# Graph attention stage: per-wave softmax work spread over more steps, three banks of sums cleared by TensorE, gathers let go one by one

## What is computed

```python
q, k, v = (h @ Wq, h @ Wk, h @ Wv)            # each (n, H, 32)
e = jnp.sum(q[dst] * k[src], axis=-1) / np.sqrt(DK)
m = jax.ops.segment_max(e, dst, num_segments=n)
a = jnp.exp(e - m[dst])
z = jax.ops.segment_sum(a, dst, num_segments=n)
alpha = a / (z[dst] + 1e-09)
msg = v[src] * alpha[:, :, None]
agg = jax.ops.segment_sum(msg, dst, num_segments=n)
```

## Time and profile before

| | |
|---|---|
| median of 3 runs | 7516.76 us |
| the profiled execution, its own time | 7514.5 us |
| span of the profile | 7512.8 us |
| PE busy (share of the span) | 5151.3 us (69%) |
| DVE busy | 2817.6 us (38%) |
| ACT busy | 1775.8 us (24%) |
| POOL busy | 2144.2 us (29%) |
| granted TensorE clock, mean | 0.795 |

### The profile page before, as it was taken

How to read it: one execution, slowest core, us unless ns; L and a number is a source line. 1 busy time by engine, 2 the same in 40 slices (tenths; PEclk the granted TensorE clock), 3 DMA queues, 4 the chain that set the end, 5 groups by cost and what they waited for, 6 DMA issues and landing times. The chain is left out here.

```text
span 7512.8 us, 86978 instructions
## 1 busy us (share of the span) xinstructions
PE 5151.3 (69%) x21926; PEld 3443.6 (46%) x21975; DVE 2817.6 (38%) x6705; ACT 1775.8 (24%) x4567; POOL 2144.2 (29%) x2209
## 2 busy tenths in 40 slices
PE   3510959659783597956666666666667969898954
PEld 2410547315681146834444444444457844444433
DVE  4260679200423004155555545555534220202052
ACT  2210236000220002214444423444422210101020
POOL 3356010540244401414444305444300410000014
PEclk7555579769796697978888778888877989999966
DMA  0000023213562133637777527777611644243323
GB/s 14 1 1 1 1 93 140 81 59 112 166 198 78 64 104 99 198 128 249 233 230 234 175 69 246 242 236 230 185 50 40 201 152 150 105 137 116 112 71 113
DMA packets 484694, 960.56 MB, mean 128 GB/s; under 512 B 112649, under 2 KB 292468, under 8 KB 481718
## 3 DMA queue, kind: packets, MB, share of 16 engines
q1 hardware_dynamic: 324902, 640.53, 25.1%
q0 software_dynamic: 114208, 281.05, 12.8%
q10 hardware_dynamic: 45296, 35.56, 1.6%
HBM read 737.19 MB, written 219.73 MB: 127 GB/s over the span
## 5 line engine op out<-in xcount | busy, mean ns | idle before, releaser
L1180 PE MATMUL banks<-ring,xn 128*128 128x512 f32 (+1 forms) x3500 | 1445.0, 568 | 397.6 <-issue 277.4
L1180 PEld LDWEIGHTS banks<-ring,xn 128*128 128x128 f32 x3500 | 644.5, 196 | 1198.8 <-issue 1182.3
L1007 POOL DMA_INDIRECT rows<-pairs,idxr x832 | 866.3, 1041 | 912.2 <-DVE prod L2022 637.0
L383 POOL DMA_INDIRECT dst_table<-nodes_pay,nodes_row x392 | 378.8, 966 | 819.9 <-DVEq L1154 479.2
L383 POOL DMA_INDIRECT bin_table<-bins_pay,bins_row x392 | 401.2, 1023 | 591.5 <-ACTq L784 205.5
L2088 PE MATMUL banks<-agg,hotT 128*128 x1664 | 527.6, 474 | 0.6 <-issue 0.6
L2121 ACT ACTIVATE x<-banks x832 | 324.6, 390 | 638.3 <-PE banks L2054 410.8
L1191 ACT ACTIVATE agg<-banks 128x512 f32<-128x512 f32 (+1 forms) x70 | 34.8, 549 | 1721.5 <-PE banks L1180 1396.2
L2088 PEld LDWEIGHTS banks<-agg,hotT 128*128 128x128 f32 x1664 | 393.6, 249 | 66.4 <-issue 1.4
L2054 PE MATMUL banks<-nodes_pay,hot 128*128 128x264 f32 x832 | 304.0, 478 | 168.6 <-ACT banks L2123 81.9
L1637 PE MATMUL banks<-xT,w1r 128*128 128x128 f32 x3088 | 403.4, 283 | 21.2 <-DVE xT L1690 9.4
(11 more groups left out here) (369 smaller groups left out, 7715.1 us busy)
## 6 DMA issues: line engine op xcount, KB each, us to landing
ring<-adjacency SPq DMA_DIRECT2D x145, 1280.0 KB
spill<-rows SPq DMA_DIRECT2D x208, 512.0 KB
vals<-spill SPq DMA_DIRECT2D x208, 512.0 KB
w1r<-in_L_ffn_W SPq DMA_DIRECT2D x114, 512.0 KB
adjacency<-strips SPq DMA_DIRECT2D x13, 3200.0 KB
w1r<-in_L_ffn_w SPq DMA_DIRECT2D x65, 512.0 KB
rows<-home_rows SPq DMA_DIRECT2D x35, 640.0 KB
ring<-adjacency SPq DMA_DIRECT2D x25, 640.0 KB
```

Of the source, the lines that this page charges most:

```text
L383: self.nc.gpsimd.indirect_dma_start(self.table, bass.IndirectOffsetOnAxis(ap=self.row[:, c:c + 1], axis=0), self.pay[:, c * W:(c + 1) * W] ...
L1007: nc.gpsimd.indirect_dma_start(rows[:, row, :], None, table, bass.IndirectOffsetOnAxis(ap=idxr[:, at + g:at + g + 1], axis=0))\
L1180: last = nc.tensor.matmul(K.ps[2 * (g % 2) + o][:, 0:wd], x[:, t * D + o * P:t * D + (o + 1) * P], ring.buffer[:, n % R, 0:wd // cols, q * ...
```

## The change

LAG goes from 8 to 9, HOTS (ring of one-hots) from 10 to 11, BEHIND from 5 to 6. There are three banks of sums (5 to 7), the query products have three banks in place of four and the small products move to bank 4. The chunk table holds four words a chunk, three of them start columns of banks, made by nine more small VectorE instructions in `number_chunks`. In the loop over steps:

- a wave's work is spread over four steps (`one` to `four`), and each engine has a new order;
- the one-hots are made a step ahead, and the first ahead of the clearing of the accumulator;
- the queries come in two halves, the second half behind `halved`, the first multiply of the step;
- ScalarE clears no bank any more: before each chunk's sum TensorE runs a matmul of zeros (1 row of bfloat16, 264 columns) over the next bank, and `kept` takes the place of `zeroed`;
- each of a group's four gathers waits for a semaphore of its own: first multiply, second multiply, one-hot (three groups later), add.

The core of the diff:

```diff
@@ gather_rows
             for g in range(half):
+                if not (isinstance(c, int) and c < 2):
+                    free, later = used[g % 4]
+                    wait_staged(pool, free, half // per * (c - 2) + g // per + 1 + later, passed)
                 if g % 4 == 0 and not (isinstance(c, int) and c < 2):
-                    wait_staged(pool, used, half // per * (c - 2) + (g + 4) // per, passed)
                     fills = c // 2 if isinstance(c, int) else 2 * k + (j - 1) // 2
                     wait_staged(pool, spilled[((j - 1) % 2 * half + g) // per], 16 * fills, passed)
@@ attention
-        zeros = st.sb("zeros", [P, W])
+        nought = st.sb("nought", [1, P + W], BF)
+        def queries(c, hh):
+            return K.ps[1 + (2 * c + hh) % 3]
-                gather_rows(nc, pool, edges, K.pairs, rows, idxr, gathered, staged, passed, product, spilled, GS)
+                gather_rows(nc, pool, edges, K.pairs, rows, idxr, gathered, staged, passed,
+                            ((halved, 0), (product, 0), (onehot, 3), (scored, 0)), spilled, GS)
@@ vector: the new order of a step
+                for i in range(S + LAG):
+                    one, two, three, four = (full(i - n) for n in range(1, 5))
+                    if four:
+                        starts = load(mybir.EngineType.DVE, edges.chunks.sums(GW * four), SUM_BANKS)
+                    if 0 <= i - 2 < S:
+                        multiply(i - 2)
+                    if two is not None:
+                        shift(two)
+                    if four:
+                        rescale(four, starts[0])
+                    if i + 1 < S:
+                        if i >= 1:
+                            dve.wait_ge(turned, i)
+                        place(i + 1)
+                    if one is not None:
+                        peaks_of_rows(one)
+                    if three:
+                        lower(three)
+                    if 0 <= i - 2 < S:
+                        score(i - 2)
+                    if 0 <= i + 1 - LAG < S:
+                        weigh(i + 1 - LAG)
+                    if one is not None:
+                        carry(one)
@@ tensor
+                    for n in range(GS):
                         k = GS * g + n
                         if k >= 2:
-                            pe.wait_ge(zeroed, k - 1)
+                            pe.wait_ge(kept, k - 1)
+                        nc.tensor.matmul(K.banks[:, bass.ds(others[n], W)], nought[0:1, 0:P], nought[0:1, P:P + W],
+                                         start=True, stop=True)
@@ tensor: the new order of a step, its waits in brackets
+   queries, first half [copied, product of two groups before]; tiles of the next step loaded
+   spread (two) [carried]; transpose of scores (one) [scored]
+   queries, second half [halved of the group before]; banks loaded
+   transposes of one-hots [onehot, copied]
+   values, four chunks [weighed, slotted, kept, rescaled]
+   move of ends (one) [ended]; factors (two) [shifted, framed]; transpose back (three) [raised, read]
@@ scalar
-                    act.wait_ge(kept, k + 1)
-                    nc.scalar.activation(bank, zeros[:, :], ACT.Copy).then_inc(zeroed, 1)
@@ scalar: the new order of a step
+   fade (two); copy of the transposes; tiles and banks loaded; exponential (two)
+   keep x4; weights (three) [returned]; slot of the next group [weighted, summed]
```

More of the change, by code:

```diff
@@ L1902, in full, with load @@
             return v if (i - 1) % GW == 0 and 0 <= v < WAVES else None
+        def load(engine, where, most):
+            _, values = nc.values_load_multi_w_load_instructions(
+                where, [engine], min_val=0, max_val=most,
+                skip_runtime_bounds_check_because="number_chunks writes tiles that there are and starts of banks of sums")
+            return values
         with nc.Block() as block:
@@ L2042, in _, with query @@
+                    if one is not None:
[8 more added lines that the diff above has]
+                        carry(one)
             @block.tensor
             def _(pe):
-                def values(g, banks, part):
+                def query(c, part, at):
+                    if part == 0:
+                        pe.wait_ge(copied, c + 1)
+                        if c >= 2:
+                            pe.wait_ge(product, c - 1)
+                    elif c >= 1:
+                        pe.wait_ge(halved, c)
+                    for n in (2 * part, 2 * part + 1):
+                        last = nc.tensor.matmul(queries(c, part)[:, n % 2 * D:(n % 2 + 1) * D],
+                                                hotT[:, c % 2, n * P:(n + 1) * P], tile_of(q, at[n]), start=True, stop=True)
+                    if part:
+                        last.then_inc(queried, 1)
@@ L2091, in _ @@
-                    if done:
-                        pe.wait_ge(framed, done)
-                        pe.wait_ge(shifted, done + 1)
-                        nc.tensor.matmul(scale, head_hot[:, :], head_fade[:, :], start=True, stop=True).then_inc(scaled, 1)
-                    if last is not None:
-                        pe.wait_ge(ended, last + 1)
+                            last = nc.tensor.transpose(turns[:, n * P:(n + 1) * P], hot[:, i % HOTS, n, :], K.ident[:, :])
+                        last.then_inc(turned, 1)
@@ L2101, in _ @@
-                    if done is not None:
-                        pe.wait_ge(raised, done + 1)
-                        if done:
-                            pe.wait_ge(read, done)
-                        nc.tensor.transpose(flat, over[:, :], K.ident[:, :]).then_inc(returned, 1)
-                    if g >= 0:
-                        values(g, banks, range(2, GS))
-                    if last is not None:
-                        pe.wait_ge(carried, last + 1)
-                        nc.tensor.matmul(spans, G.of_headT[:, :], past[:, :, :].rearrange("p w b -> p (w b)"), start=True,
-                                         stop=True).then_inc(spread, 1)
+                    if two is not None:
+                        pe.wait_ge(shifted, two + 1)
+                        if two:
+                            pe.wait_ge(framed, two)
+                            nc.tensor.matmul(scale, head_hot[:, :], head_fade[:, :], start=True, stop=True).then_inc(scaled, 1)
@@ new lines, in _ @@
+                    if three is not None:
+                        act.wait_ge(returned, three + 1)
+                        if three >= 2:
+                            act.wait_ge(weighed, GW * (three - 1))
+                            act.wait_ge(slotted, GW * (three - 1))
+                        nc.scalar.activation(weights[:, three % 2, :], flat, ACT.Copy).then_inc(weighted, 1)
+                    if 0 <= g + 1 < S:
+                        slot(g + 1)
+                act.wait_ge(kept, CHUNKS)
```

254 lines of the change are left out of this document (120 added, 134 removed).

## The result

The changed kernel takes 7322.44 us (median of 4 runs, 7313.93 to 7327.7), the kernel before 7516.23 us beside it. The ratio is 0.9741, with a 95% interval of 0.9725 to 0.9758: faster by 194 us, where 375 were forecast. The time lies 2 us above the range.

A forecast was written before the change was run, and what follows sets the result against it. It took two chains as the bound: the wave's round trips, and TensorE with ScalarE over two banks; next, DMA. Steps -181 and -178, tails -18, starts -4, numbering +5 make -376, from 7514.5 to 7138, as median 7141 us; range 7015 to 7320.

The forecast's parts named there:

- The four waits of a wave: VectorE idle before peaks, factors, spread maxima and rescaling in the kernel before: 14.0 us a wave, forecast close to nothing.
- The wait for the weights: VectorE's first weighing of a wave waits for weights that TensorE and ScalarE deliver behind the values: 2.8 us.
- 28.0 us a wave: Forecast length of a wave of four steps, taken between the transfers' 26.4 and 28.9 us; 35.0 before.
- The matmul of zeros, 0.15 us a chunk: TensorE's cost of clearing a bank before each chunk's sum: between nothing and 0.25 us, 2.4 us a wave.
- TensorE's steps: A step of TensorE forecast at 5.2 to 5.6 us, against 4.2 for a plain step of VectorE.
- DMA as the bound: Transfers of 8.3 MB a wave at 314 to 287 GB/s need 26.4 to 28.9 us, above the engines' 25.5.
- The engines' bound: A wave's time by VectorE's work and remaining waits and TensorE's longer steps: 25.5 us.
- Gathers let go singly: Each of a wave's sixteen gathers waits for its own semaphore: 19.8 us a wave, under 28, so counted as nothing.
- The rival in which POOL becomes the bound: All sixteen gathers pay 0.98 us behind their semaphores, 30.9 us a wave: 7290 us, chance 0.10.
- Tails, -18, and starts, -4: Both rounds: tail after the last one-hot falls from 72 to 63 us; each start before the first one-hot saves 2.
- The waits move: Rival: each step costs a TensorE-VectorE round trip, steps stay near 8 us, 32 us a wave: 7347 us, chance 0.17.
- The clock: Rival: short stops in every step bring TensorE's clock down to 0.62, 37.9 us a wave: 7650 us, chance 0.05.

The follow-up runs named there:

- the narrow one: Changed kernel with the zeroing matmul over 8 columns in place of 264: 6359.36 us, 0.9449 of the kernel before, in the faster pace.
- e_best: Changed kernel with transpose back and weights ahead of the values, four gathers released together, zeroing over 8 columns: 6254.86 us, 0.9296 of the kernel before, faster pace.
- e_narrow: Changed kernel with the zeroing matmul over 8 columns in place of 264, first run: 6356.31 us, 0.9448 of the kernel before, faster pace.
- e_narrow2: Changed kernel with the zeroing matmul over 8 columns in place of 264, run again beside its control: 6359.36 us, 0.9449 of the kernel before.
- e_best2: Changed kernel with early transpose back and weights, four gathers released together, zeroing over 8 columns, slower pace: 7233.78 us, 0.9634 of the kernel before.

## Where the prediction was right and where it was wrong

**Right.** The four waits of a wave were the cost, and they went, though in a third of their time VectorE waited for nothing that the profile shows, and not for a round trip. The wait for the weights was named as what is left, and is the largest. The gathers are hardly ever late, and ScalarE holds TensorE for only 20.1 / 22.5 = 0.9 us a wave: its copies come 0.86 us apart (0.73 forecast), mostly set by TensorE. `number_chunks` ends at 962.49 in place of 958.00, 4.5 us for the 5 forecast.

**Wrong: 28.0 us a wave, which is 31.2.** Of the 181 us between forecast and result, 163 lie in the 206 steps, forecast at 721 us a round, and the rest in tails and starts. VectorE works 20.1 us a wave, as before; its idle time is 11.0 us where some 4 to 5 were forecast, and 2.0 of that have no releaser in the profile. The steps of the sum that failed:

*The matmul of zeros, 0.15 us a chunk.* The row it was sized by was a train of seven bfloat16 matmuls of one kind. None of them stands between float32 sums, and 0.25 us was taken for the most it could be. The row even ran at half the clock (0.50 in the window of the kernel before that stands below), so for the columns alone the 0.25 us was plenty, twice the 0.12 us of a second zeroing. What the price left out is the train of sums that the zeroing breaks up:

```profile
939.60:942.10 2.50, 2.47 (x8) 0.72 (x6) 0.00 (x0) 0.00 (x0) 1.89 (x3) 0.50 0.02 1
```

It costs 0.4 to 0.5 us. 16 x 0.25 to 0.35 is 4.0 to 5.6 us more work a wave on TensorE, whose busy time is 605 / 22.5 = 26.9 us where 22.5 to 24 was forecast. The text had "a matmul of zeros takes over 0.3 us" among what would prove it wrong; counted by what it costs a chunk, that is what came. How much of the 3.2 us a wave goes back to it no run shows alone, since no run takes the zeroing off TensorE without giving it to ScalarE; the narrow one gives back 71 / 51.5 = 1.4 us in the faster pace.

*The wait for the weights, 2.8 us a wave.* It is 5.6. The chain to it runs over the four chunks of values on TensorE, and those were taken at 3.2 us, with the cheap zeroing and at full clock; at 0.85 us a chunk they are 3.4.

*TensorE's steps.* As these came out longer than VectorE's, the carry (forecast 0.7 to 1, measured 2.3) and the one-hot (forecast nothing, measured 2.0) wait for TensorE too.

*DMA as the bound.* It was forecast at 26.4 to 28.9 us a wave, above the engines' 25.5. The engines' bound was too low, so it was not reached: share 0.82, and cutting traffic gave 18 us. In e_best, with the engines' costs down and in the faster pace, the wave came to 25.9 us at 321 GB/s and a share of 0.94, so the size was about right; whether the transfers hold the wave there is open. The Trainium skill's ceiling of about 358 GB/s (DMA: Bandwidth & Descriptors, Specifications) was reached in no stretch shown here.

*Gathers let go singly, counted at nothing.* It costs 37 us in the slower pace, by a way that is not known. The rival in which POOL becomes the bound forecast a smaller gain, but by another mechanism, and POOL is busy 471 of 810 us.

*Tails, -18, and starts, -4.* From the last one-hot to the last copy are 79.7 and 79.3 us where 63 was forecast, 16 us more than before in both rounds together. The columns of some forty zeroings are 8 us a tail of it, at a clock of 0.64. The starts, with the one-hots a step ahead, gave back 20 us; with the numbering the three come to about nothing where -17 was forecast.

**The rivals.** *The waits move* (7347) came nearest in time, and half of it happened: TensorE's second query half waits for VectorE's first multiply, 41.9 us in 22.5 waves, and VectorE's one-hot for TensorE's values. But that is one stop of some 2 us a wave, not a round trip in every step. *The clock* did not fall below its old value (0.88 after 0.85), so there was no loss, yet it did not rise to 1 either; filling one of the stops went with a gain of 29 us. The Trainium skill's rule (TensorE: Matmul & The Clock Gate, "A second HAM failure mode") agrees with that in kind: a mean of 0.88 is time at both levels, by estimate 2 x 0.12 x 31.2 = 7.5 us a wave at 1.2 GHz, and 2 x 0.15 x 35.0 = 10.5 before. The rival was dismissed by one plain step of the trace of before; the wave's step was the one to look at.

## What to carry to other kernels

An instruction that the trace does not have is to be priced between the neighbours it will have, not in a train of its own kind: here breaking up a train of sums cost more than the one-row matmul that did it. Where waits are taken off an engine that works little more than half of the time (VectorE, 518 of 902 us), the next bound is the other busy engine with everything the change adds to it, so each term put on it needs an upper end. And parts that ride along with a large change deserve a run alone: the single release of the gathers cost 37 us under a gain of 194.

## What the runs showed of the hardware

- A zeroing matmul of one bfloat16 row between float32 sums sets the chunk at 0.85 us (264 columns) or 0.80 us (8 columns), and a second one adds only 0.12 us. The next matmul behind a sum starts 0.64 to 0.65 us later, be it the bfloat16 zeroing or a small float32 product; in a train of sums the next chunk starts after 0.34 to 0.45 us. The 8 columns reopen the bank as 264 do (e_narrow, e_narrow2).
- The same program runs at two paces, 7516 and 6722 us for the kernel before, and the change is worth 2.6% at one and 4.4% at the other. Chip number 10 has both on record. In e_best and e_best2 the granted clock in the stage is 0.96 and 0.87 and the DMA rate 321 and 281 GB/s. The cause was not found.
- Two useless matmuls a wave in a stop of TensorE made the kernel 29 us faster.
